# The products of layers 1 and 2 made in two instructions of 1024 columns, with tails of the groups before between them

## The reference

```
e = stack of 40 table rows                      # [512, 40, 32]
h = e
for W, b in three layers (200 maps each):
    x = einsum('bhd,bmd->bhmd', h, e).reshape(B, -1, 32)
    y = relu(einsum('oi,bid->bod', W, x) + b)   # W0: 200 x 1600, W1 and W2: 200 x 4000
    h, direct = split(y, 2)                     # the last layer: direct = y
z = concat(all direct).sum(-1)                  # [512, 400]
h = relu(concat(z, dense_ctx) @ W_top1 + b1); h = relu(h @ W_top2 + b2)
y = h @ W_top3                                  # [512, 1]
```

## Time and profile before

| | |
|---|---|
| median of 3 runs | 2819.57 us (2819.26 to 2823.86) |
| the profiled execution | 2822.93 us, its span 2821.1 us |
| PE busy in the span | 2775.4 us, 98% |
| DVE busy | 2637.9 us, 94% |
| ACT busy | 1500.6 us, 53% |
| POOL busy | 858.7 us, 30% |
| mean granted TensorE clock | 0.998 |
| chain that ended last | PE 94%, POOL 2%, DVE 1%, DMA 1% |

### The profile page before, as it was taken

One profiled execution on the slowest core, in us unless ns is written; L12 is line 12 of the kernel. 1 busy time (PEld: TensorE's weight loads), 2 busy tenths in 40 slices (PEclk: granted clock), 3 DMA queues, 4 the chain that ended last, 5 costly groups with the idle time before them and its releaser, 6 DMA issues.

```text
span 2821.1 us, 54038 instructions
## 1 busy us (share of the span) xinstructions
PE 2775.4 (98%) x19012; PEld 2758.2 (98%) x19012; DVE 2637.9 (94%) x1945; ACT 1500.6 (53%) x1880; POOL 858.7 (30%) x700
## 2 busy tenths in 40 slices
PE   5999999999999999999999999999999999999999
PEld 4999999999999999999999999999999999999997
DVE  6999999999999999999999999999999999999995
ACT  4555555555555555555555555555555555555553
POOL 5433332332332332332323323323323323333100
PEclk9999999999999999999999999999999999999999
DMA  7333333433433433333334334334333334334330
GB/s 210 85 83 84 86 94 78 94 87 76 99 88 75 100 84 82 97 84 85 93 79 94 87 78 97 89 75 102 85 78 99 85 82 95 85 86 94 85 78 18
DMA packets 286025, 249.66 MB, mean 89 GB/s; under 512 B 31286, under 2 KB 284446, under 8 KB 285893
## 3 DMA queue, kind: packets, MB, share of 16 engines
q1 hardware_dynamic: 216310, 200.56, 25.4%
q0 software_dynamic: 65712, 45.56, 12.1%
q10 hardware_dynamic: 3972, 3.17, 0.4%
HBM read 140.74 MB, written 4.20 MB: 51 GB/s over the span
## 4 chain that ended last, share of the span: by engine, by line
PE 94%; POOL 2%; DVE 1%; DMA 1%; issue 1%; SPq 0%; ACT 0%; another core or an unknown queue 0%; DVEq 0%; ACTq 0%; POOLq 0%
PE acc L809 62%; PE acc L811 29%; POOL gathered L445 1%; PE z_ps L826 1%; PE hid_ps L822 1%; DVE tails L721 1%; DMA acc_copy<-acc_copy 1%; DVE product L716 1%; PE acc L880 0%; SPq L380 0%; DMA gathered<-in_table,rows_all 0%; PE hid_ps L903 0%; DMA hid_rep<-hid 0%; ACT acc_copy L528 0%
## 5 line engine op out<-in xcount | busy, mean ns | idle before, releaser
L809 PE MATMUL acc<-weights,heads 126*128 126x400 f32 (+1 forms) x9088 | 2694.1, 364 | 16.3 <-DVE tails L721 16.2
L811 PE MATMUL acc<-weights,tails 126*128 126x200 f32 (+1 forms) x9088 | 2321.6, 255 | 0.0
L522 ACT ACTIVATE heads<-product 126x1024 fp32r<-126x1024 f32 (+2 forms) x1152 | 1198.1, 1047 | 1021.5 <-PE acc L811 507.3
L811 PEld LDWEIGHTS acc<-weights,tails 126*128 126x128 f32 (+1 forms) x9088 | 1740.8, 192 | 0.0
L809 PEld LDWEIGHTS acc<-weights,heads 126*128 126x128 f32 (+1 forms) x9088 | 1712.9, 188 | 19.7 <-issue 10.0
L721 DVE TENSOR_TENSOR tails<-product,heads 126x1024 fp32r<-126x1024 f32 (+2 forms) x1152 | 1348.9, 1204 | 1.4 <-ACT heads L522 1.1
L716 DVE TENSOR_TENSOR product<-hid_rep,x_rep 126x2048 f32<-126x2048 f32 x510 | 1167.4, 2289 | 96.5 <-PE acc L811 64.8
L453 POOL DMA_DIRECT2D acc_copy<-acc_copy x189 | 235.0, 1244 | 1719.8 <-ACT acc_copy L528 1716.4
L445 POOL DMA_INDIRECT gathered<-in_table,rows_all x320 | 510.8, 1596 | 101.4 <-issue 97.1
L536 ACT ACTIVATE y_relu<-acc_copy 128x400 f32<-128x400 f32 x192 | 102.4, 533 | 217.0 <-DMA acc_copy<-acc_copy 215.0
L528 ACT ACTIVATE acc_copy<-acc 128x800 f32<-128x800 f32 x192 | 158.7, 827 | 9.8 <-PE acc L811 7.7
(11 more groups left out here) (26 smaller groups left out, 118.2 us busy)
## 6 DMA issues: line engine op xcount, KB each, us to landing
x_rep<-x_rows SPq DMA_DIRECT2D x512, 120.0 KB
hid_rep<-hid SPq DMA_DIRECT2D x511, 120.0 KB
x_pairs<-x_rows SPq DMA_DIRECT2D x191, 280.0 KB
acc_copy<-acc_copy POOLq DMA_DIRECT2D x189, 200.0 KB
hid_rep<-hid SPq DMA_DIRECT2D x511, 5.0 KB
x_pairs<-x_rows SPq DMA_DIRECT2D x63, 120.0 KB
gathered<-in_table,rows_all POOLq DMA_INDIRECT x320
raw_weights<-in_w SPq DMA_DIRECT2D x8, 500.0 KB, 6.1
```

Of the source, the lines that this page charges most:

```text
L522: act.activation(heads[0:rows, ring % HEADS_RING, 0:tiles, :], product[0:rows, ring % PRODUCT_RING, 0:tiles, :], ACT.Copy).then_inc(heads_ ...
L809: nc.tensor.matmul(acc[:, at.parity, c, 0:2 * LAYER], dims(heads[0:rows, ring % HEADS_RING, k, :], c), w, start=(q == 0 and k == 0), stop= ...
L811: last = nc.tensor.matmul(acc[:, at.parity, c, LAYER:2 * LAYER], dims(tails[0:rows, ring % PRODUCT_RING, k, :], c), w[:, 0:LAYER], start=F ...
```

## The change

make_products gets a function to call between two halves. For layers 1 and 2 each pair of groups is made by two instructions of 1024 columns, one a group. Each has a wait of its own, groups_used >= g - 5 for the first and g - 4 for the second, and each signals products_made by 1. Between the halves stand the tails of the first group of the pair before; the fold, where there is one, and the tails of the second group follow behind. Layer 0's products stay as they were.

```
@@ make_products
+                if layer == 0:
+                    above_zero(dve, groups_used, g - (PRODUCT_RING - 2))
                     ...
+                        dve.tensor_tensor(out, first, second, ALU.mult).then_inc(products_made, 2)
                     return
-                above_zero(dve, groups_used, g - (PRODUCT_RING - 2))
-                dve.tensor_tensor(out, first, second, ALU.mult).then_inc(products_made, 2)
+                for n in range(2):
+                    above_zero(dve, groups_used, g + n - (PRODUCT_RING - 1))
+                    dve.tensor_tensor(out[:, n:n + 1], first[:, n:n + 1], second[:, n:n + 1], ALU.mult).then_inc(products_made, 1)
+                    if n == 0 and between_halves:
+                        between_halves()
@@ make_previous_tails
-                make_tails(layer, q, g - 2, (ring - 2) % RING)
+                if not first_made:
+                    make_tails(layer, q, g - 2, (ring - 2) % RING)
@@ step
-                        make_products(layer, at, q, i - layer, parity)
+                        halves = None
+                        if previous[0] and layer > 0:
+                            def halves(last=previous[0], g=at.group + q - 2, ring=(at.ring + q - 2) % RING):
+                                make_tails(last[0], last[1], g, ring)
+                        make_products(layer, at, q, i - layer, parity, halves)
...
-                            make_previous_tails(at.group + q, at.ring + q, between)
+                            make_previous_tails(at.group + q, at.ring + q, between, halves is not None)
```

More of the change, by code:

```diff
@@ L681, in _, with make_products @@
             split_tails(*split_after("start"))
-            def make_products(layer, at, q, b, parity):
+            def make_products(layer, at, q, b, parity, between_halves=None):
                 g, place0 = at.group + q, (at.ring + q) % PRODUCT_RING
@@ L709, in make_products @@
                     second = x_rep[0:rows, parity, half * GROUP:(half + 1) * GROUP, :].unsqueeze(1).to_broadcast(shape)
-                above_zero(dve, groups_used, g - (PRODUCT_RING - 2))
[L711 to L714, removed]
-                    return
-                dve.tensor_tensor(out, first, second, ALU.mult).then_inc(products_made, 2)
+                if layer == 0:
+                    above_zero(dve, groups_used, g - (PRODUCT_RING - 2))
+                    if isinstance(b, int) and b == 0:
+                        for a, z in ((0, GROUP), (GROUP, TILES0)):
+                            dve.tensor_tensor(out[:, a:z], first[:, a:z], second[:, a:z], ALU.mult).then_inc(products_made, 1)
+                    else:
+                        dve.tensor_tensor(out, first, second, ALU.mult).then_inc(products_made, 2)
+                    return
+                for n in range(2):
[3 more added lines that the diff above has]
+                        between_halves()
             def make_tails(layer, q, g, ring):
@@ L741, in fold, with make_previous_tails @@
                                   ALU.add).then_inc(y_folded, 1)
-            def make_previous_tails(g, ring, between=None):
+            def make_previous_tails(g, ring, between=None, first_made=False):
                 layer, q = previous[0]
-                make_tails(layer, q, g - 2, (ring - 2) % RING)
+                if not first_made:
+                    make_tails(layer, q, g - 2, (ring - 2) % RING)
                 if between:
```

## The result

The changed kernel takes 2829.01 us in the median of 20 runs (2821.29 to 2867.01), the kernel before beside it 2819.41 us (20 runs, 2814.34 to 2829.72). The ratio is 1.0042 with a 95% interval of 1.0028 to 1.0055 (the ratios here are not quotients of the medians, which would give 1.0034). The change makes the kernel slower by 9.6 us where 2.3 us less was forecast, and the time lies outside the range. Its runs also lie far apart, 46 us against 15 (28 us without the longest of them, which counts as a slow one). The profiled run of after took 2849.03 us with a span of 2847.2, 26.1 us above that of before; it is one of the long ones.

What follows compares the result with a forecast made beforehand. TensorE was taken to bound the kernel, VectorE a close second. Added instructions and finer waits 0, start -2.4, end +0.1: -2.3 us, from the median 2819.57 to 2817.3 us; range 2812 to 2824 us.

Steps and rivals of the forecast that it cites:

- The added instructions: 8 pairs of each block split: +0.07 us a pair, 0.6 us a block, covered by VectorE's idle time; path cost 0.
- The two rules weighed there: On VectorE, fixed latency per operation and waiting for an empty pipe: 0.16 to 0.24 us more a pair.
- The start: Before 200 us, tails behind less product work shrink gaps at 55.72, 80.37 and 136.67: -2.4 us, bounds 0 and -4.
- The finer waits: In the loop, first halves wait for an earlier group; thinnest margin grows from 0.4 to 2.4 us, gain 0.
- The queues: At the end, SP's loads of 2765.38 come 1.2 us later, +0.1 us net; other engines keep their order.
- rival 2: Start gives nothing and late signals to SP's loads take it back: 2818 to 2823 us, no change; chance 0.25.
- The gap at 676.50: In the loop, TensorE waited 0.87 us for tails behind a layer 0 product resumed 2.62 us late; left as is.
- rival 1: In the loop, halves cost more than VectorE has free: at 0.30 us a pair, 2849 us; chance 0.09.

Runs made afterwards that it cites:

- few gaps: Changed kernel, VectorE waiting for its own product behind the last two pairs of layer 2 in every block and of layer 1 in block 0: 2824.34 us.
- the first version with gaps: Changed kernel, VectorE waiting for its own product behind the third and fourth pair of layer 2: 2829.99 us, ratio 1.0032.
- after with all gaps: Changed kernel, VectorE waiting for its own product behind every written-out second half and two layer 2 pairs in the loop: 2817.77 us, ratio 1.0001.
- run 0: Not a label of any run: the words belong to "costs a run 0 to 7 us", the stall's cost in any one run.
- the kernels made for this: Three separate kernels, no reference output: GpSimd gathers beside gapless VectorE streams; in one, first gathers 4.9 and 9.4 us behind a gap took 1.68 and 18.71 us.
- two other versions: Changed kernel with the first half waiting as long as the second, 2827.95 us; or with both tails behind both halves, 2826.72 us.

## Why the prediction was wrong, point by point

The prediction says 2817.3 us, in a range of 2812 to 2824; measured were 2829.01. The steps that failed are the third and the fourth below.

- **The added instructions: right.** 1219 ns each, covered: with the gaps put back TensorE is busy for 2500.00 of 2500 us with all halves in place, and without gathers the change is a gain of 1.9 us. The two rules weighed there, on a fixed cost and on an empty pipe, have no part in the loss: tails and halves start 1.14 us apart (2023.33 and 2024.47) and last 1.22.
- **The start, a gain of 2.4 us: right in mechanism, and lost.** Without the loop's gathers, after did 1066 matmuls from 28 to 200 us and before 1057, 9 more, 1.3 us. With the gathers, the two long ones of the start turned it into a loss of 7.8 us in the profiled run.
- **The finer waits: the step that failed.** The prediction says that a wait of VectorE for TensorE "costs nothing by itself". True, and read as if such a wait were also worth nothing. These waits (161 of them) were GpSimd's openings. From 200 to 2700 us VectorE has 324 pieces of over 0.03 us without work before and 146 after, in nearly the same total (2500 - 2385.38 = 114.6 and 2500 - 2381.53 = 118.5 us); the longest run without one grew from 27 to 41 us. Free time went from many small pieces into few large ones, and the sum of it, on which the prediction leaned, hid that.
- **The queues: the other half of it.** "ScalarE, TensorE, POOL and SP keep their order": so they do. But order isn't duration, and no step of the prediction asked how long GpSimd's instructions take and what is queued behind them. The profile of before showed it: the gathers at 1596 ns, with the one of 11.12 us behind which the fold of 131.77 waited 2.77 us. What the queue cost is in the chain above: 24.01 us of gather, 9.90 us of TensorE.
- **Late loads (rival 2): seen, harmless.** Waits for x_rep rose from 16 to 38; with the gaps put back there are 28 of them and TensorE loses nothing.
- **The gap at 676.50: right about the place, and a stall that comes and goes.** The prediction left it as it was, in front of the unsplit layer 0 product. There it stays, but at other times: after has it once, the product of 2069.25 held for 4.51 us and TensorE for 2.19 at 2072.47; the profile of few gaps has it four times (products held for 2.43 to 3.92 us), that of the first version with gaps three times (2.10 to 3.46 us, TensorE at 771.50, 900.79 and 1802.29). The kernel before with gaps in its written-out steps, and after with all gaps, have none, with TensorE busy for 2500.00 us. So it costs a run 0 to 7 us, beside the gathers; its cause stays open.
- **The chances.** No case had this mechanism. The case on the slower side had another one, with 0.09, and the range ended at 2824. That rival 1 names 2849 us, and the profiled run took 2849.03, is luck: it told of instructions that last too long.

## What to carry to other kernels

Before making VectorE's stream smoother, look at what GpSimd does beside it: a gather that reads its indices in SBUF may depend on the pieces of free time that the change removes, and everything queued behind it on GpSimd waits too. Don't count free time by its sum alone, but by its pieces and the longest run without one. Where a stream must be dense, a wait of VectorE for its own last result, 0.03 us of gap, shortly before the gather comes is a cheap way to let it through; here such waits, two in each block of the loop and one behind every second half in the written-out steps, took the 9.6 us of loss away and cut the spread of the runs from 46 to 1.6 us.

## What the runs showed of the hardware

- A gather on GpSimd beside gapless two-input instructions on VectorE was held for up to 28.2 us, over 24 instructions, not for one; in the changed kernel all 60 gathers of over 3 us later than 50 us ended 0.92 to 0.96 us after VectorE's next gap began (2025.69 to 2026.63), and a gap of 0.03 us was enough.
- Up to 5.8 us behind such a gap, or just behind another gather, it passed in 1.1 to 2.1 us beside the same instructions; 9.4 us and more behind it was held in the kernels made for this and in after. 14 gathers of two other versions passed 20 to 32 us behind the last gap, ten of them beside a start of VectorE that was 0.01 to 0.08 us late.
- An accumulating DMA issued by GpSimd passed beside two-input products 29 us behind VectorE's last gap (1.31 us) and was held for 13.60 us, until their end, by copies of one input, at the end of a stream of 24 copies of 0.61 us each (14.54 us).
- No complete version measured here beats the kernel before by more than can be measured: the nearest, the kernel before with gaps in its written-out steps, stands at 0.9996 (0.9987 to 1.0005). The gathers' whole cost in it is some 3.5 us.
